# Sixteen groups instead of twelve gathered while the table is built; GpSimd's tensor operations there moved to ScalarE and VectorE

## The reference

```python
h = relu(layernorm(x))                                  # 12500 x 128
cat = concatenate((h[src], h[dst], edge_attr), axis=-1)  # 200000 x 384
msg = relu(cat @ W1 + b1)                               # 200000 x 128
aggr = segment_sum(msg, dst, num_segments=12500)
out = x + gamma * normalise(aggr + h) + beta            # layernorm over 128
```

## Time and profile before

| | |
|---|---|
| median of 3 runs | 2785.59 us |
| lowest, highest | 2776.02, 2791.99 us |
| span of the profiled execution | 1998.5 us |
| rest, median less span | 787.1 us |
| TensorE, VectorE, ScalarE, GpSimd busy | 84%, 42%, 42%, 75% of the span |

### The profile page before, as it was taken

The page is one execution under the profiler, slowest core; times in us unless marked ns, Lnnn a source line. Parts: engine busy times, 40 slices in busy tenths (PEclk is TensorE's granted clock), DMA queues, the critical chain, the costliest instruction groups (busy, mean ns, idle before and its releaser), DMA issues.

```text
span 1998.5 us, 51574 instructions
## 1 busy us (share of the span) xinstructions
PE 1675.0 (84%) x13397; PEld 1619.2 (81%) x13397; DVE 847.0 (42%) x2958; ACT 832.9 (42%) x1853; POOL 1501.5 (75%) x1579
## 2 busy tenths in 40 slices
PE   5788889888897888888798788888888888888886
PEld 5688888788887887888787788887888778878786
DVE  7534444444344443444444343343333344334434
ACT  5544444444444444444443343343343334334333
POOL 7777777777777777777777777777777777777775
PEclk9798988898899899899899998999899899999988
DMA  9544444444444444454444444444444444444442
GB/s 267 164 126 120 125 123 125 122 135 114 131 123 122 120 132 125 114 138 121 122 135 111 123 129 117 114 128 122 113 130 115 120 118 130 116 123 125 110 129 74
DMA packets 208223, 252.43 MB, mean 126 GB/s; under 512 B 43789, under 2 KB 132341, under 8 KB 208197
## 3 DMA queue, kind: packets, MB, share of 16 engines
q1 hardware_dynamic: 136756, 139.76, 23.9%
q0 software_dynamic: 50048, 102.60, 20.6%
q10 hardware_dynamic: 21392, 9.77, 1.7%
HBM read 229.38 MB, written 22.59 MB: 126 GB/s over the span
## 4 chain that ended last, share of the span: by engine, by line
POOL 37%; issue 25%; DMA 16%; PE 14%; DVEq 4%; DVE 2%; POOLq 1%; ACT 0%; ACTq 0%; SPq 0%
POOL a_rows L523 34%; DMA a_rows<-table_a,picks 15%; PE ps_pre L683 4%; PE ps_pre L684 4%; DVEq L1209 3%; POOL aggr L486 2%; PE ps_edge L664 2%; PE ps_hot L671 2%; PE ps_sum L694 1%; PE ps_fin L694 1%; DVE msg L1205 1%; POOLq L530 0%; PE ps_sum L701 0%; DVEq L1202 0%; DVE e_norm L1237 0%
## 5 line engine op out<-in xcount | busy, mean ns | idle before, releaser
L523 POOL DMA_INDIRECT a_rows<-table_a,picks x1516 | 1445.1, 953 | 464.5 <-issue 417.8
L906 ACT ACTIVATE msg<-msg 128x512 f32<-128x512 f32 x391 | 246.4, 630 | 1037.8 <-DVE msg L1205 1029.6
L1205 DVE TENSOR_TENSOR msg<-ps_pre,a_rows 128x512 f32<-128x512 f32 x391 | 270.5, 692 | 927.5 <-DMA a_rows<-table_a,picks 643.4
L683 PE MATMUL ps_pre<-w_c,edge_cols 128*128 128x128 f32 x3128 | 650.9, 292 | 0.0
L684 PE MATMUL ps_pre<-b_win,onehot_cols 128*128 128x128 f32 x3128 | 645.3, 290 | 0.0
L683 PEld LDWEIGHTS ps_pre<-w_c,edge_cols 128*128 128x128 f32 x3128 | 522.3, 210 | 0.0
L684 PEld LDWEIGHTS ps_pre<-b_win,onehot_cols 128*128 128x128 f32 x3128 | 517.8, 208 | 0.0
L671 PE MATMUL ps_hot<-ident,onehot 128*128 128x128 f32 x1564 | 262.7, 295 | 11.2 <-DVE onehot L1186 11.2
L694 PE MATMUL ps_sum<-onehot,msg 128*128 128x64 f32 x1568 | 207.3, 276 | 72.4 <-ACT msg L906 69.0
L694 PEld LDWEIGHTS ps_sum<-onehot,msg 128*128 128x128 f32 x1568 | 196.6, 197 | 82.6 <-ACT msg L906 78.4
L664 PE MATMUL ps_edge<-ident,edges 128*128 128x128 f32 x1564 | 259.0, 292 | 1.5 <-ACT dst_f L819 1.4
(11 more groups left out here) (123 smaller groups left out, 1062.8 us busy)
## 6 DMA issues: line engine op xcount, KB each, us to landing
edges<-in_edge_attr SPq DMA_DIRECT2D x391, 256.0 KB
a_rows<-table_a,picks POOLq DMA_INDIRECT x1516
b_win<-table_b SPq DMA_DIRECT2D x391, 32.0 KB
out<-out_rows SPq DMA_DIRECT2D x97, 64.0 KB
table_b<-b_rows ACTq DMA_DIRECT2D x96, 64.0 KB
x_all<-in_x SPq DMA_DIRECT2D x13, 448.0 KB, 5.8
table_a<-a_out SPq DMA_DIRECT2D x13, 448.0 KB, 4.0
table_early<-e_rows ACTq DMA_DIRECT2D x48, 64.0 KB
```

The costliest lines, as they stand in the source:

```text
L523: pool.indirect_dma_start(a_rows[:, u, k, :], None, table_a[:, :], bass.IndirectOffsetOnAxis(ap=picks[:, u, k:k + 1], axis=0),).then_inc(s ...
L683: pe.matmul(to, edge_cols[:, u % 2, k * P:(k + 1) * P], w_c[:, :], start=True, stop=False)
L906: act.activation(msg[:, u % 2, :, :], msg[:, u % 2, :, :], ACT.Relu).then_inc(s_msg, 1)
L1205: dve.tensor_tensor(msg[:, u % 2, :, :].rearrange("p k f -> p (k f)"), ps_pre[u % 2][:, :], a_rows[:, u, :, :].rearrange("p k f -> p (k f) ...
```

## The change

`EARLY` goes from 8 to 6, so 16 groups (64 blocks) are gathered early and every sixth round has one; `EARLY_AT` goes from `AHEAD + 3` to `AHEAD + 1`. The row numbers come by ScalarE's queue in two transfers, the first group's by itself. POOL's memset of x's padding, its diagonal and its addition to `b_first` go to VectorE (the last fused with the scaling, which ScalarE did), its casts to ScalarE. VectorE waits for all early gathers after its first two one-hots, not before the branch. As 64 is no multiple of 6, VectorE's loop gets a piece for the rounds 60 to 65.

```diff
-EARLY = 8
+EARLY = 6
-    EARLY_AT = AHEAD + 3
+    EARLY_AT = AHEAD + 1
+    EARLY_REST = EARLY_ROWS % EARLY
@@ sync
-            sp.dma_start(early_picks[:, :, :],
-                         src[...].rearrange(...)[:, :, EARLY * UNROLL - 1, :]).then_inc(s_early_picks, 16)
@@ gpsimd
-            pool.memset(x_all[:, BLOCKS - 1:ALL_BLOCKS, :], 0.0).then_inc(s_pad, 1)
+            pool.wait_ge(s_first_picks, 16)
+            pool.sem_inc(s_gate_pool, 1)
+            gather_early(0)
             pool.wait_ge(s_early_picks, 16)
-            pool.sem_inc(s_gate_pool, 1)
-            for s in range(EARLY_GROUPS - 3):
+            for s in range(1, EARLY_GROUPS):
                 gather_early(s)
-            pool.wait_ge(s_ids[0], ID_LOADS * 16)
-            for q in range(2):
-                pool.tensor_copy(ids_f[0:ROWS, 0, q, :], ids_i[0:ROWS, 0, q, :]).then_inc(s_cast[0], 1)
-            for s in range(EARLY_GROUPS - 3, EARLY_GROUPS):
-                gather_early(s)
-            pool.wait_ge(s_range, 1)
-            pool.tensor_tensor(diagonal[0:ROWS, :, 0:ROWS], ...).then_inc(s_diag, 1)
-            pool.wait_ge(s_b_first_kept, 1)
-            pool.wait_ge(s_weights, 80)
-            pool.tensor_tensor(b_first[:, :, :], b_first[:, :, :], ..., ALU.add).then_inc(s_b_first_kept, 1)
@@ scalar
+            act.dma_start(early_picks[:, 0, :], early_src[:, 0, :]).then_inc(s_first_picks, 16)
+            act.dma_start(early_picks[:, 1:, :], early_src[:, 1:, :]).then_inc(s_early_picks, 16)
@@ scalar, for the last two chunks
                 keep_a(c - 2, c % 2, c // 2 - 1)
+                cast_ids(0, (c - CHUNKS + 2) * 2, (c - CHUNKS + 3) * 2)
-            act.wait_ge(s_b_first, 1)
-            for k in range(AHEAD):
-                ins = act.activation(b_first[:, k, :], ..., ACT.Copy, scale=scale_all[:, k:k + 1])
-            ins.then_inc(s_b_first_kept, 1)
@@ vector
+            dve.memset(x_all[:, BLOCKS - 1:ALL_BLOCKS, :], 0.0).then_inc(s_pad, 1)
@@ vector, after scale(CHUNKS - 1)
+            dve.wait_ge(s_const, 5)
+            dve.wait_ge(s_range, 1)
+            dve.tensor_tensor(diagonal[0:ROWS, :, 0:ROWS], ..., ALU.mult).then_inc(s_diag, 1)
@@ vector, after the first four picks
+            dve.wait_ge(s_b_first, 1)
+            dve.wait_ge(s_weights, 80)
+            dve.wait_ge(s_scale, CHUNKS)
+            for k in range(AHEAD):
+                ins = dve.scalar_tensor_tensor(out=b_first[:, k, :], in0=ps_first[...], scalar=scale_all[:, k:k + 1],
+                                               in1=b1_all[:, :], op0=ALU.mult, op1=ALU.add)
+            ins.then_inc(s_b_first_kept, 1)
@@ vector, loop
-            dve.wait_ge(s_early_raw, EARLY_ROWS * 16)
                 one_hot(0, 0)
                 one_hot(0, 1)
+                dve.wait_ge(s_early_raw, EARLY_ROWS * 16)
-                with dve.Fori(EARLY_ROWS // EARLY, EARLY_GROUPS) as s:
+                half = EARLY_ROWS // EARLY
+                with dve.Fori(EARLY_ROWS - EARLY_REST, EARLY_ROWS) as i:
+                    round_(i, i - half + 1, early=True)
+                with dve.Fori(EARLY_ROWS, half * EARLY + EARLY - 1) as i:
+                    round_(i, i - half + 1)
+                round_(half * EARLY + EARLY - 1, None, loaded=half + 1)
+                with dve.Fori(half + 1, EARLY_GROUPS) as s:
                     rounds(s, False)
```

More of the change, by code:

```diff
@@ L74, in build @@
     assert E % SUB == 0 and FULL_GROUPS == GROUPS - 1 and ID_ROWS == GROUPS + 1 and ROWS <= P
-    assert EARLY_GROUPS * EARLY == ROUNDS - 2 and 3 + SUB < EARLY and EARLY_ROWS % EARLY == 0
+    assert EARLY_GROUPS * EARLY == ROUNDS - 2 and SUB + 1 < EARLY and 0 < EARLY_REST < EARLY - 1
     assert EARLY_AT + EARLY_ROWS <= ALL_BLOCKS - 2 * QUADS * SUB
@@ L195, in build @@
         s_pad = sem("s_pad")
+        s_count = sem("s_count")
         s_const = sem("s_const")
@@ L258, in build @@
         s_out_stored = sem("s_out_stored")
+        s_first_picks = sem("s_first_picks")
         s_early_picks = sem("s_early_picks")
@@ L364, in _ @@
             load_x(0, 0)
-            sp.dma_start(early_picks[:, :, :],
-                         src[0:EARLY_GROUPS * EARLY * UNROLL * GROUP].rearrange(
-                             "(s g p k) -> p s g k", s=EARLY_GROUPS, g=EARLY * UNROLL, p=P)[:, :, EARLY * UNROLL - 1, :]
-                         ).then_inc(s_early_picks, 16)
             load_x(1, 1)
@@ L477, in _ @@
                                base=0, pattern=[[-1, P]], channel_multiplier=1).then_inc(s_const, 1)
-            pool.memset(x_all[:, BLOCKS - 1:ALL_BLOCKS, :], 0.0).then_inc(s_pad, 1)
             pool.iota(count[:, :], pattern=[[1, WIDE]], base=0, channel_multiplier=0,
-                      allow_small_or_imprecise_dtypes=True).then_inc(s_pad, 1)
+                      allow_small_or_imprecise_dtypes=True).then_inc(s_count, 1)
             def gather_early(s):
@@ L489, in gather_early @@
                     ).then_inc(s_early_raw, 16)
+            pool.wait_ge(s_first_picks, 16)
+            pool.sem_inc(s_gate_pool, 1)
+            gather_early(0)
             pool.wait_ge(s_early_picks, 16)
-            pool.sem_inc(s_gate_pool, 1)
-            for s in range(EARLY_GROUPS - 3):
+            for s in range(1, EARLY_GROUPS):
                 gather_early(s)
-            pool.wait_ge(s_ids[0], ID_LOADS * 16)
-            for q in range(2):
-                pool.tensor_copy(ids_f[0:ROWS, 0, q, :], ids_i[0:ROWS, 0, q, :]).then_inc(s_cast[0], 1)
-            for s in range(EARLY_GROUPS - 3, EARLY_GROUPS):
-                gather_early(s)
-            pool.wait_ge(s_range, 1)
[L501 to L504, removed]
-            pool.wait_ge(s_b_first_kept, 1)
-            pool.wait_ge(s_weights, 80)
-            pool.tensor_tensor(b_first[:, :, :], b_first[:, :, :],
-                               b1_all[:, :].unsqueeze(1).to_broadcast([P, AHEAD, H]), ALU.add
-                               ).then_inc(s_b_first_kept, 1)
             pool.wait_ge(s_planned, 1)
@@ L622, in _ @@
             mm.then_inc(s_plan, 1)
-            pe.wait_ge(s_cast[0], 3)
             turn_ids(0, 1)
+            pe.wait_ge(s_cast[0], 2)
             for a in range(2):
@@ L780, in _ @@
         def _(act):
+            early_src = src[0:EARLY_GROUPS * EARLY * UNROLL * GROUP].rearrange(
+                "(s g p k) -> p s g k", s=EARLY_GROUPS, g=EARLY * UNROLL, p=P)[:, :, EARLY * UNROLL - 1, :]
+            act.dma_start(early_picks[:, 0, :], early_src[:, 0, :]).then_inc(s_first_picks, 16)
+            act.dma_start(early_picks[:, 1:, :], early_src[:, 1:, :]).then_inc(s_early_picks, 16)
             act.wait_ge(s_const, 5)
@@ L809, in keep_a, with cast_ids @@
                 ins.then_inc(s_a_kept[1], 1)
-            def cast_ids(a, first):
+            def cast_ids(a, first, end):
                 act.wait_ge(s_ids[a], ID_LOADS * 16)
-                act.activation(ids_f[0:ROWS, a, first:, :], ids_i[0:ROWS, a, first:, :], ACT.Copy
+                act.activation(ids_f[0:ROWS, a, first:end, :], ids_i[0:ROWS, a, first:end, :], ACT.Copy
                                ).then_inc(s_cast[a], 1)
@@ L825, in _ @@
             h_columns(0, 0)
-            cast_ids(1, 0)
+            cast_ids(1, 0, QUADS)
             for c in range(1, 4):
@@ L841, in _ @@
                 keep_a(c - 2, c % 2, c // 2 - 1)
+                cast_ids(0, (c - CHUNKS + 2) * 2, (c - CHUNKS + 3) * 2)
             for c in range(CHUNKS - 2, CHUNKS):
                 keep_a(c, c % 2, c // 2)
-            act.wait_ge(s_b_first, 1)
-            for k in range(AHEAD):
-                ins = act.activation(b_first[:, k, :], ps_first[k // 4][:, (k % 4) * H:(k % 4 + 1) * H],
-                                     ACT.Copy, scale=scale_all[:, k:k + 1])
-            ins.then_inc(s_b_first_kept, 1)
[L849 to L852, removed]
+            keep_ids(0, src_f, 0, range(QUADS))
+            act.wait_ge(s_b_first_kept, 1)
             act.dma_start(table_b[0:AHEAD * P, :].rearrange("(b p) f -> p b f", p=P), b_first[:, :, :]
@@ L1090, in _ @@
             scale(CHUNKS - 1)
+            dve.wait_ge(s_const, 5)
+            dve.wait_ge(s_range, 1)
+            dve.tensor_tensor(diagonal[0:ROWS, :, 0:ROWS],
+                              ident[0:ROWS, 0:ROWS].unsqueeze(1).to_broadcast([ROWS, QUADS, ROWS]),
+                              lowest[0:ROWS, :].unsqueeze(2).to_broadcast([ROWS, QUADS, ROWS]), ALU.mult
+                              ).then_inc(s_diag, 1)
             for q in range(2):
@@ L1097, in _ @@
             ins.then_inc(s_range, 1)
-            dve.wait_ge(s_const, 5)
             dve.wait_ge(s_range, 2)
@@ L1116, in _ @@
                 pick(0, u)
+            dve.wait_ge(s_b_first, 1)
+            dve.wait_ge(s_weights, 80)
+            dve.wait_ge(s_scale, CHUNKS)
+            for k in range(AHEAD):
+                ins = dve.scalar_tensor_tensor(out=b_first[:, k, :],
```

(8 more changed lines are left out.)

## The result

The changed kernel took 2803.84 us (median of 10 runs, 2792.32 to 2811.89), the kernel before 2782.72 (10 runs, 2774.26 to 2798.91): ratio 1.0065, 95% interval 1.0042 to 1.0088, 12 to 25 us slower. Forecast were 2779.5 us, a range of 2767 to 2793, and no change.

What follows compares the result with a forecast made beforehand. POOL's serial gathers were taken to bound the kernel. Terms -0.1 - 2.2 - 1.0 - 3.4 + 0.4 + 0.2 = -6.1 us gave 2785.6 - 6.1 = 2779.5 us, range 2767 to 2793.

Steps and rivals of the forecast that it cites:

- 787.1 us are outside the span: Timed median 2785.59 us less profiled span 1998.5 us; taken as unchanged by the change.
- a scaling by 1.39: Alternative: everything in the timed runs longer in proportion, saving 8.5 us, time 2777.1 us.
- The prediction's own last sign of being wrong: Prediction wrong if the span falls by over 10 us, or if the 787 us outside it change.
- POOL bounds the loop: Loop: POOL issues 1516 gathers at 1.258 us each without one stall, and their number sets the end.
- Step 1: Sixteen gathers move from loop (20.1 us) to the end of table building (20.0 us): net -0.1 us.
- Step 7: Loop: sixteen more rounds prepare early rows; TensorE waits for e_norm in each, POOL does not notice: nothing.
- Table building ends near 67 us: Start: table building is over near 67 us, so the later early gathers run clean at 1.25 us each.
- steps 3, 4 and 8: Table building: casts leave POOL, -1.0 us; gap before loop shrinks, -3.4; VectorE's later wait for early gathers hidden.
- Step 2: Start: row numbers land sooner, first early gather at 4.4 us instead of 6.61: -2.2 us.
- Step 4: Between last early gather and loop: 5.20 us shrink to 1.80 for reading the flag and branching: -3.4 us.
- Step 5: Table building: diagonal on VectorE stretches one gather issued beside it: +0.4 us, bounds 0 and +0.9.
- Rival B: Loop: TensorE becomes the bound as slack does not return within six rounds, 1.5 us per visit: 2803 us; chance 0.09.

Runs made afterwards that it cites:

- A: Regime: series of runs in which the kernel before takes 1996 to 2003 us; the profile that the prediction read came from it.
- B: Regime: series of runs in which the kernel before takes 2760 to 2842 us; the timed runs before and the result came from it.
- experiment 3: Changed kernel with EARLY = 8 (twelve early groups), rest of the change kept; in B 2808.30 us, ratio 0.9979 to before; second series 2772.58 us, 0.9976.
- experiment 5: Changed kernel without early groups, every group's rows gathered in the loop; in A 2051.51 us, ratio 1.0252 to before; in B 2706.52 us, 0.9721.

## Why the prediction was wrong

The step that failed is "787.1 us are outside the span and no row shows them. I take them as unchanged." They were inside the span of every timed run; 1.8 to 2.0 us are outside it. A profiled execution of 1998.5 us and timed runs of 2785.59 were not one state of the machine, and a rest of 28% should have been made a rival with a large chance, not a constant. Only a scaling by 1.39 was considered, which kept the sign. The prediction's own last sign of being wrong, that the 787 us change, is what came.

By its own steps:

- *POOL bounds the loop*: right in A (longest wait 0.3 us again), false in B (788.5 us for picks, longest 11.5).
- *Step 1, sixteen gathers move at equal price, +20.0 and -20.1.* In A the loop's first gather came at 90.5 for 91.9 forecast, its last at 1976.1 for 1977.6. In B the first half holds: from 12 to 16 groups, start 114.7 to 137.3, +22.6. The second half is missing. The addition of round 96 follows that of round 0 by 2602.9 us with twelve groups (experiment 3, second series) and by 2598.8 with sixteen (the change): 4 us gained for the 20.1 forecast. With the sixteen groups alone the loop even grew, against experiment 3 in the same series, by 8.6 us in one and by 23.8 in the other. These are single executions, and those of one kernel in one series spread by 4 to 32 us, so the sizes are rough; no pair shows a gain near 20. Why: rounds whose early group needs no gather are shorter, but the sixteen rounds that prepare rows are longer. The change's rounds take 27.6 us up to round 63 and 26.0 after it, those of before 27.8 and 26.8; without early rows they are 26.9 throughout (experiment 5). Step 7's "Nothing" is thus 1.0 to 1.6 us a round, 16 to 26 us, in B. Start and loop sum to about +19 in the first pair of traces, beside the +21 of the medians.
- *Table building ends near 67 us beside the gathers*, the cover of steps 3, 4 and 8: right in A; in B it ends some 50 us after the last early gather.
- *Step 2, the first row numbers*: 4.53 for 4.4, in both regimes (4.55 in B). 
- *Step 4, what remains between early gathers and loop*: 0.31 us of idle in A, for 1.80 taken; the bound of 0.30 was the truth. That is most of the difference between 6.1 forecast and 7.8 in the spans of A.
- *Step 5, the diagonal beside gathers*: no cost, for +0.4 taken. In A the diagonal ran on VectorE at 63.77 for 0.60 us, and the gather issued with it took 0.94. The early gathers together came out as the steps had them: they started every (89.27 - 4.53)/63 = 1.345 us. The Trainium skill's port rule (page "SBUF — State Buffer", section "SBUF: two separate sides") is about VectorE and GpSimd blocking each other, and says of TensorE and ScalarE that they "never wait on anyone" there. In B ScalarE stood 44.6 us and the gathers stayed at 0.95, so that rule does not explain B.
- *Rival B* had the right side, near 2803, and its sign (POOL waiting over 0.3 us for picks) was seen, but not its mechanism: TensorE does not run out of clock, it fails to start instructions while POOL gathers, as half the gathers show. That its 2803 meets the measured 2803.84 is luck: its +24 stood for slack lost at 16 visits of a loop bound by POOL, and it had the loop start 14 us later; in B it started 23.7 later (113.63 to 137.28).

Shown: gathers, not POOL's time, hold the other engines up in B; it costs the start as above; the sixteen groups carry the whole loss; neither the DMA engines' bandwidth nor the clock is what is short. Not shown: through what. TensorE's instructions start one by one, mostly 1.4 us apart, with no wait in front, and ScalarE stands with its work ready. That looks like instructions or semaphore updates that come late; no run here separates the two. No run put plain transfers from another queue in place of the gathers, so whether only indirect ones do this is open too. Nor is it known what puts a series into A or B; none of the experiments could choose it.

No version wins in both: with no early groups 0.9721 in B and 1.0252 in A, the change 1.0065 and 0.9967.

## What to carry to other kernels

Compare the profile's span with the timed runs before reading a row of it. Here 1.8 to 2.0 us belonged outside it; a rest of 787 meant that the trace showed another regime, and a sum made from it did not forecast the timed one. An engine's idle time is not free to fill: ask what else has to go on while it works, and measure the moved work alone, in the regime that is timed. When two regimes exist, a change should be judged in each.

## What the runs showed of the hardware that was not expected

- One program, 51574 instructions, 1998.5 or 2799.0 us by series. The mean granted clock of TensorE was 0.922 in the first and 0.793 in the second.
- In the second regime, back-to-back indirect gathers of 128 rows (0.95 us and a gap of 0.30) let TensorE start one instruction in 1.4 us, mostly, for some 22 us, and left ScalarE standing for up to 44.6 us with its input written; 120 iotas of POOL did not delay table building. The DMA engines were 0.30 busy meanwhile, for 0.77 in the first regime.
- Halving the gathers of the kernel without early groups took 41% off its time in that regime (2706.52 to 1589.36 us) and 27% in the other (2051.51 to 1498.14).
